# The end of an attention and FFN block: output products of one step inside the next step's softmax, and the last norm in two pairs of tiles

## What is computed

```
Q = norm(x) @ Wq.T        K = ctx @ Wk.T        V = ctx @ Wv.T      (8 groups of 4 query heads)
scores = Q K * 128**-0.5, causal over 64 positions; probs = softmax(scores)
x = x + tanh(g_xattn) * (probs @ V) @ Wd.T
w = (unpacked 6-bit qweight - zero_point) * scale
x = x + tanh(g_ffn) * (norm(x) @ w.T + bias)
norm(x) = (x - mean) / sqrt(var + 1e-5), over 512 features
```

## Time and profile before

| | |
|---|---|
| median of three executions | 1109.43 us |
| the profiled execution, and its span | 1111.87 us, 1110.1 us |
| mean granted TensorE clock | 0.986 of 2.4 GHz |
| TensorE busy | 1043.2 us, 94% of the span |
| VectorE busy | 717.6 us, 65% |
| ScalarE busy | 487.9 us, 44% |
| GpSimd busy | 238.3 us, 21% |

### The profile page before, as it was taken

The page is one execution under the profiler, slowest core; times in us unless marked ns, Lnnn a source line. Parts: engine busy times, 40 slices in busy tenths (PEclk is TensorE's granted clock), DMA queues, the critical chain, the costliest instruction groups (busy, mean ns, idle before and its releaser), DMA issues.

```text
span 1110.1 us, 20245 instructions
## 1 busy us (share of the span) xinstructions
PE 1043.2 (94%) x8054; PEld 589.1 (53%) x8054; DVE 717.6 (65%) x1347; ACT 487.9 (44%) x937; POOL 238.3 (21%) x242
## 2 busy tenths in 40 slices
PE   5899999998999999999999999999999999999974
PEld 3455545554455555455555555555555555555532
DVE  6856666567667666665566676656567656655567
ACT  5756674684624334244435323254433532333322
POOL 1535564457513110110002110110000300000012
PEclk9999999999999999999999999999999999999987
DMA  7746545432462342333222443322233233331101
GB/s 265 235 144 248 202 145 168 142 124 98 130 210 79 132 148 100 114 115 114 90 78 82 171 153 114 115 81 63 105 115 115 96 115 114 115 115 58 58 19 57
DMA packets 64251, 137.10 MB, mean 124 GB/s; under 512 B 5408, under 2 KB 38176, under 8 KB 53536
## 3 DMA queue, kind: packets, MB, share of 16 engines
q1 hardware_dynamic: 64160, 135.81, 35.8%
HBM read 93.85 MB, written 25.17 MB: 107 GB/s over the span
## 4 chain that ended last, share of the span: by engine, by line
PE 79%; DVE 9%; ACT 5%; issue 3%; POOL 0%; DVEq 0%; ACTq 0%; POOLq 0%
PE pa L1127 34%; PE py L1127 30%; PE av L1234 5%; PE ps L1201 3%; PE py L1284 3%; PE pp L1217 2%; PE av L1269 1%; DVE sc L838 1%; DVE row_max L842 1%; DVE sc L844 1%; ACT junk L537 1%; DVE sc L855 1%; DVE q L798 1%; ACT pT L636 1%; ACT junk L547 1%
## 5 line engine op out<-in xcount | busy, mean ns | idle before, releaser
L1127 PE MATMUL pa<-xT,wq 128*128 128x512 f16 x1536 | 347.3, 380 | 7.9 <-DVE q L798 5.2
L1127 PE MATMUL py<-wd,att 128*128 128x512 f16 x1536 | 351.4, 381 | 0.9 <-ACT att L643 0.9
L1127 PEld LDWEIGHTS pa<-xT,wq 128*128 128x128 f16 x1536 | 144.2, 98 | 180.3 <-issue 20.9
L1127 PEld LDWEIGHTS py<-wd,att 128*128 128x128 f16 x1536 | 149.0, 99 | 164.8 <-issue 5.2
L877 DVE SCALAR_TENSOR_TENSOR xacc<-py,f_y,xacc 128x512 f32<-128x512 f32 x128 | 96.1, 750 | 160.8 <-PE py L1127 160.8
L598 ACT ACTIVATE q<-pa 128x512 f16<-128x512 f32 x128 | 75.7, 592 | 248.2 <-PE pa L1127 248.2
L643 ACT ACTIVATE att<-av 128x256 f16<-128x256 f32 x256 | 80.9, 385 | 160.7 <-PE av L1234 160.3
L868 DVE SCALAR_TENSOR_TENSOR att<-av,att 128x256 f16<-128x256 f32 x256 | 93.5, 416 | 78.7 <-ACT att L643 78.6
L798 DVE SCALAR_TENSOR_TENSOR q<-pa,q 128x512 f16<-128x512 f32 x128 | 87.4, 683 | 20.6 <-ACT q L598 20.6
L1127 PE MATMUL pa<-wv,cT 128*128 128x128 f16 x1536 | 96.2, 219 | 0.0
L1127 PEld LDWEIGHTS pa<-wv,cT 128*128 128x128 f16 x1536 | 89.8, 98 | 0.9
(11 more groups left out here) (110 smaller groups left out, 1103.2 us busy)
## 6 DMA issues: line engine op xcount, KB each, us to landing
wq<-kept_q SPq DMA_DIRECT2D x24, 1024.0 KB, 7.9
wd<-kept_d SPq DMA_DIRECT2D x24, 1024.0 KB, 4.8
v_dup<-v_nat SPq DMA_DIRECT2D x128, 128.0 KB, 2.4
raw_d<-in_wdT SPq DMA_DIRECT2D x8, 1024.0 KB, 8.4
kept_q<-wq SPq DMA_DIRECT2D x8, 1024.0 KB, 8.8
kept_d<-wd SPq DMA_DIRECT2D x8, 1024.0 KB, 4.8
raw_q<-in_wqT SPq DMA_DIRECT2D x7, 1024.0 KB, 5.3
wk<-kept_k SPq DMA_DIRECT2D x24, 256.0 KB, 7.7
```

The lines of the kernel that those rows point to most:

```text
L1127: last = pe.matmul(out, stationary(a, i), moving(b, i), start=(i == 0 and (a, b) == PASSES[0]), stop=(i == count - 1 and (a, b) == PASSES[ ...
```

## The change

Step 30 no longer runs its output products (y_unit, y_part); they stand between the parts of step 31's softmax on TensorE and VectorE. Step 31's own output weights get a place of their own, wd_last (the second half of raw_d), and a load of their own (back_d_last), issued ahead of back_d(30). The FFN units of block 2 (LATE, tiles 8 to 11) use the banks pa instead of py, and their scaled products go to xs (the second half of raw_q) instead of xn; two stand in step 31 around the attention units, two behind its last output product. The last norm is done in two pairs of tiles (ln_stats_of, rstd_here with a slice), the first pair between output products 1 and 2 of step 31. ScalarE, POOL and the transpositions and FFN units of block 3 go by the same pairs; the stores of block 2 and 3 stand together at the end of SyncE's list. The core of the diff (indentation cut by eight):

```diff
+xs = raw_q[:, 1, :, :, :].rearrange("p h k n -> p h (k n)")
+wd_last = raw_d[:, 1, :, :].rearrange("p h n -> p (h n)").bitcast(F16).rearrange(
+    "p (c h n) -> p c h n", c=2, h=HPG)
...
+LAST = STEPS - 1
+LATE = tuple(range((BLOCKS - 2) * TILES, (BLOCKS - 1) * TILES))
 def ffn_of(n):
     g, tb = n % GROUPS, n // GROUPS
-    if n == STEPS - 1:
-        return BLOCKS - 2
     if g == 1 and 0 < tb < BLOCKS - 1:
         return tb - 1
...
+    def back_d_last():
+        sp.wait_ge(wd_lo, 4 * GROUPS)
+        sp.dma_start(wd_last.rearrange("p c h n -> p (c h n)"), kept_d[GROUPS - 1]).then_inc(d_last, 16)
...
+        if n == LAST - 1:
+            back_d_last()
+        if GROUPS <= n < LAST:
             back_d(n)
...
-    for t in FFN_DVE:
+    for t in LATE + FFN_DVE:
...
         pool.wait_ge(xr_ok, t + 1)
         pool.wait_ge(f_scaled, t + 1)
-        pool.tensor_tensor(acc(t), acc(t), xn[:, t % TILES, :], ALU.add).then_inc(out_pool, 1)
+        part = xs[:, t % TILES, :] if t in LATE else xn[:, t % TILES, :]
+        pool.tensor_tensor(acc(t), acc(t), part, ALU.add).then_inc(out_pool, 1)
...
-    for t in FFN_DVE:
-        residual(t)
+    for pair in (0, 2):
+        for t in LATE[pair:pair + 2]:
+            ffn_add(t)
+        for t in FFN_DVE[pair:pair + 2]:
+            residual(t)
...
-    for t in range(t0, t0 + TILES):
-        ln_hi(t, True)
-    for t in range(t0, t0 + TILES):
-        ln_out(t)
+    for pair in (t0, t0 + 2):
+        for t in (pair, pair + 1):
+            ln_hi(t, True)
+        for t in (pair, pair + 1):
+            ln_out(t)
...
+    def ln_stats_of(call, pair):
+        before = 4 * call + 2 * pair
+        two = slice(pair, pair + 2)
+        for t in (pair, pair + 1):
+            dve.wait_ge(bn_ok, TILES * call + t + 1)
+            dve.bn_aggr(mv[:, t, :], bn[:, t, :]).then_inc(mv_ok, 1)
+        dve.wait_ge(mv_ok, TILES * call + pair + 2)
+        dve.tensor_scalar(var_e[:, two], mv[:, two, 1], LN_EPS, None, ALU.add).then_inc(seed_ok, 1)
+        dve.tensor_scalar(half_var[:, two], mv[:, two, 1], LN_EPS, -0.5, ALU.add, ALU.mult).then_inc(seed_ok, 1)
+        dve.wait_ge(seed_ok, before + 2)
+        dve.tensor_scalar(rs_bits[:, two], var_e[:, two].bitcast(I32), 1, None,
+                          ALU.logical_shift_right).then_inc(seed_ok, 1)
+        dve.wait_ge(seed_ok, before + 3)
+        dve.tensor_scalar(rs[:, 0, two].bitcast(I32), rs_bits[:, two], -1.0, float(RSQRT_MAGIC),
+                          ALU.mult, ALU.add).then_inc(seed_ok, 1)
+        dve.wait_ge(seed_ok, before + 4)
+    def rstd_here(before, at):
         count = before
...
+        if 1 < call < len(NORMS) - 1 and NORMS[call - 1][0] == 2:
             dve.wait_ge(out_pool, NORMS[call - 1][1] * TILES + at + 1)
-        if call == len(NORMS) - 1:
-            dve.wait_ge(out_pool, (BLOCKS - 2) * TILES + at + 1)
...
-        dve.tensor_tensor(xn[:, t % TILES, :], py[t % 2][:, :], ff_rows[:, SCALE_ROW, :],
+        bank, part = (pa, xs) if t in LATE else (py, xn)
+        dve.tensor_tensor(part[:, t % TILES, :], bank[t % 2][:, :], ff_rows[:, SCALE_ROW, :],
                           ALU.mult).then_inc(f_scaled, 1)
...
-            y_part(n, j)
+            if n < LAST - 1:
+                y_part(n, j)
             if g == GROUPS - 1:
...
+    n, last = LAST, len(NORMS) - 1
+    scores(n, 0)
+    y_part(n - 1, 0)
+    scores(n, 1)
+    normalise(n, 0)
+    y_part(n - 1, 1)
+    p_part(n, 0)
+    normalise(n, 1)
+    y_part(n - 1, 2)
+    p_part(n, 1)
+    y_part(n - 1, 3)
+    ffn_scaled(LATE[0])
+    av_part(n, 0)
+    av_part(n, 1)
+    ffn_zero(LATE[0])
+    ffn_scaled(LATE[1])
+    ffn_zero(LATE[1])
+    y_part(n, 0)
+    ln_bn(last, 0)
+    av_part(n, 2)
+    y_part(n, 1)
+    ln_bn(last, 1)
+    av_part(n, 3)
+    ln_stats_of(last, 0)
+    rstd_here(10, slice(0, 2))
+    ln_norm(TILES * last)
+    ln_norm(TILES * last + 1)
+    y_part(n, 2)
+    ln_bn(last, 2)
+    ln_lo(TILES * last)
+    ln_lo(TILES * last + 1)
+    y_part(n, 3)
+    ln_bn(last, 3)
+    ln_stats_of(last, 2)
+    rstd_here(20, slice(2, 4))
+    ln_norm(TILES * last + 2)
+    ln_norm(TILES * last + 3)
+    ffn_scaled(LATE[2])
+    ffn_scaled(LATE[3])
+    ln_lo(TILES * last + 2)
+    ln_lo(TILES * last + 3)
+    ffn_zero(LATE[2])
+    ffn_zero(LATE[3])
+    for pair in (0, 2):
+        for t in FFN_DVE[pair:pair + 2]:
+            ffn_zero(t)
+        for t in FFN_DVE[pair:pair + 2]:
+            ffn_scaled(t)
+            ffn_result(t)
...
+            elif n == LAST:
+                pe.wait_ge(d_last, 16)
...
-                lambda b, h: wd[:, b, h, :], HPG).then_inc(y_mm, 1)
+                lambda b, h: (wd_last if n == LAST else wd)[:, b, h, :], HPG).then_inc(y_mm, 1)
...
-        pe.wait_ge(y_ok, min(4 * n, 4 * STEPS))
+        if t == LATE[0]:
+            pe.wait_ge(k_hi, STEPS)
+            pe.wait_ge(k_lo, STEPS)
+        elif t == LATE[1]:
+            pe.wait_ge(v_hi, STEPS)
+            pe.wait_ge(v_lo, STEPS)
+        elif t not in LATE:
+            pe.wait_ge(y_ok, 4 * n)
         wait(pe, f_scaled, t - 1)
...
+        bank = pa if t in LATE else py
...
+        if n == LAST - 1:
+            av_unit(n, 2)
+            av_unit(n, 3)
+            continue
...
+    n, t0 = LAST, TILES * (len(NORMS) - 1)
+    score_unit(n, 0)
+    y_unit(n - 1, 0)
+    score_unit(n, 1)
+    y_unit(n - 1, 1)
+    y_unit(n - 1, 2)
+    p_transpose(n, 0)
+    y_unit(n - 1, 3)
+    p_transpose(n, 1)
+    ffn_unit(LATE[0], n)
+    av_unit(n, 0)
+    av_unit(n, 1)
+    ffn_unit(LATE[1], n)
+    y_unit(n, 0)
+    av_unit(n, 2)
+    y_unit(n, 1)
+    av_unit(n, 3)
+    y_unit(n, 2)
+    y_unit(n, 3)
+    ffn_unit(LATE[2], n)
+    ffn_unit(LATE[3], n)
+    for pair in (0, 2):
+        ln_transpose(t0 + pair, 4 * STEPS)
+        ln_transpose(t0 + pair + 1, 4 * STEPS)
+        ffn_unit(FFN_DVE[pair], STEPS)
+        ffn_unit(FFN_DVE[pair + 1], STEPS)
```

More of the change, by code:

```diff
@@ L147, in build @@
         q_back, k_back, v_back, d_back = pair("q_back"), pair("k_back"), pair("v_back"), sem("d_back")
+        d_last = sem("d_last")
         ff_ld = sem("ff_ld")
@@ L917, in rstd_here @@
                 for i in range(3):
-                    y = rs[:, i, :]
-                    chained(dve.tensor_tensor(rs_t[:, :], y, half_var[:, :], ALU.mult))
-                    chained(dve.tensor_tensor(rs_u[:, :], rs_t[:, :], y, ALU.mult))
+                    y = rs[:, i, at]
+                    chained(dve.tensor_tensor(rs_t[:, at], y, half_var[:, at], ALU.mult))
+                    chained(dve.tensor_tensor(rs_u[:, at], rs_t[:, at], y, ALU.mult))
                     if i < 2:
-                        chained(dve.scalar_tensor_tensor(out=rs[:, i + 1, :], in0=rs_u[:, :], scalar=1.5, in1=y,
+                        chained(dve.scalar_tensor_tensor(out=rs[:, i + 1, at], in0=rs_u[:, at], scalar=1.5, in1=y,
                                                          op0=ALU.add, op1=ALU.mult))
-                chained(dve.tensor_scalar(rs_u[:, :], rs_u[:, :], 1.5, XN_SCALE, ALU.add, ALU.mult))
-                chained(dve.tensor_tensor(rstd[:, :], rs_u[:, :], rs[:, 2, :], ALU.mult))
+                chained(dve.tensor_scalar(rs_u[:, at], rs_u[:, at], 1.5, XN_SCALE, ALU.add, ALU.mult))
+                chained(dve.tensor_tensor(rstd[:, at], rs_u[:, at], rs[:, 2, at], ALU.mult))
             def ln_norm(t):
@@ L1031, in _ @@
             dve.wait_ge(const_ok, 3)
-            for n in range(STEPS):
+            for n in range(LAST):
                 g, tb, m = n % GROUPS, n // GROUPS, n + 1
-                ahead = m < STEPS
                 call = norm_of(n)
@@ L1047, in _ @@
                         split_wq(1, h)
-                if ahead:
-                    q_part(m, 0)
-                if ffn is not None and not ahead:
-                    ffn_scaled(t0)
+                q_part(m, 0)
                 scores(n, 1)
                 normalise(n, 0)
-                if ahead:
-                    q_part(m, 1)
+                q_part(m, 1)
                 if ffn is not None:
-                    ffn_scaled(t0 if ahead else t0 + 1)
+                    ffn_scaled(t0)
                 p_part(n, 0)
                 normalise(n, 1)
-                if ahead:
-                    q_part(m, 2)
+                q_part(m, 2)
                 if ffn is not None:
-                    ffn_scaled(t0 + 1 if ahead else t0 + 2)
+                    ffn_scaled(t0 + 1)
                 p_part(n, 1)
-                if ahead:
-                    q_part(m, 3)
+                q_part(m, 3)
                 if ffn is not None:
-                    ffn_scaled(t0 + 2 if ahead else t0 + 3)
-                if ffn is not None and ahead:
+                    ffn_scaled(t0 + 2)
                     ffn_scaled(t0 + 3)
-                if ahead:
-                    k_part(m)
+                k_part(m)
                 if call is not None and g == 0:
@@ L1104, in _ @@
                     ln_stats(NORMS.index((1, tb + 1)))
```

(14 more changed lines are left out.)

49 lines of the change are left out of this document (14 added, 35 removed).

## The result

The changed kernel takes 1095.4 us (median of 4; 1092.9 to 1095.56) against 1109.43 (median of 4), a ratio of 0.9867 with a 95% interval of 0.9849 to 0.9884: 14.0 us, 1.3% faster. The forecast was 1094.2 (range 1091.2 to 1099.0). Run once more beside the experiments it took 1095.73 against 1110.51, ratio 0.9865 (0.9850 to 0.9880).

What follows compares the result with a forecast made beforehand. TensorE, busy 94% of the span, left about 20 us idle and some lower clock in the last 60 us. VectorE's last instruction moves from 1107.66 to 1092.5, so 1109.43 - 15.2 = 1094.2 us, range 1091.2 to 1099.0.

Steps and rivals of the forecast that it cites:

- The softmax stretch: Step 31 on TensorE: step 30's products fill the softmax waits, so the last output product ends 14.0 us earlier, at 1068.1.
- FFN unit 12's wait: TensorE at the end: 5.4 us idle for unit 10's f_scaled, then unit 12 at 1.2 GHz, 3.41 us.
- The norm in pairs: Last norm on VectorE: ten small instructions paid twice, 2 us more work, with VectorE the bound of the new end.
- Contention: End of the kernel: POOL's two adds and two residuals slow VectorE's ffn_zero and ffn_result by 2.3 us.
- rival (a): End of the kernel: all six POOL instructions hold VectorE, 6.4 instead of 3.4 us; 3.0 later, 1097.2 us; chance 0.20.
- Two chains of nearly one length: End of the kernel: TensorE's chain leads to an end at 1091.0, VectorE's to 1092.5 with POOL's slowing.
- The sum: Whole end: VectorE's last instruction moves from 1107.66 to 1092.5, 15.2 us less, last store unchanged behind it.
- (b): Step 31's softmax isn't covered: TensorE waits 2 us more and the clock falls; 5 to 6 later, 1099.5 us; chance 0.13.
- (c): End of the kernel: the 10.5 us of idle time only move and nothing is gained, 1109.4 us; chance 0.03.
- (d): Clock falls in step 31's softmax and stays low to the end: 15.2 gained, 19.5 lost, 1113.7 us; chance 0.02.
- The waits for d_last, k and v: Step 31 on TensorE: added waits for the extra weight load and for units 8 and 9's inputs cost 0.

Runs made afterwards that it cites:

- the filler: 24 unused matmuls put in TensorE's four softmax waits, against the kernel with step 30's output products back in step 30: 1105.98 us, 0.9950 of the kernel before.
- POOL cut: Changed kernel with POOL's last four instructions working on one column instead of 512, other columns left out: 1093.50 us, 0.9845 of the kernel before.
- early ffn_zero: Changed kernel with block 2's four ffn_zero together in VectorE's pause before FFN unit 8's result: 1095.00 us, 0.9855 of the kernel before.
- again: The changed kernel, nothing further altered, run once more beside the experiments: 1095.73 us, 0.9865 of the kernel before.

## Why the prediction was right, point by point

- **The softmax stretch: right.** Forecast: last output product 14.0 us earlier, ended at 1068.1, or 1067.4 with the 0.69 us by which this profile entered the stretch earlier; measured 1067.31 (the next product starts at 1067.15). Counted from the yardstick it is 14.1 us earlier, 30.98 instead of 45.10. I had TensorE waiting about 1.0 us, 0.8 of it for p_part 0; it waited 0.31, with 2.4 GHz throughout as taken. That the gain is idle time and clock, and the products' place its cause, is shown: putting the products back costs 12.5, the filler returns 1.9 of it. As in the forecast, 3.5 us are the two FFN units put behind.
- **FFN unit 12's wait: right.** 5.4 us forecast, 5.33 measured; the two units at 5.7 against 5.83.
- **The norm in pairs: right that it costs a second chain and that VectorE is the bound of the new end.** The chain of statistics took 2.92 us (1063.78 to 1066.70) against 2.85 taken. What the text didn't say is how little the pairs bring on top of the moved products: 0.33 us of stretch.
- **Contention: right in the sum, not in its parts.** 2.3 taken, 2.58 measured, and 0.91 for ln_lo (2.20 - 1.29) against 1.1. I took 2.3, above the middle, because ffn_result is of the kind of ln_lo, and had no row for ffn_zero. It came the other way round: ffn_result lost only 0.28 each (0.56 in all), and ffn_zero 2.02, as two of four took 1.75 us instead of 0.75. That 2.3 comes so near is in part luck. The rule of the Trainium skill (page "SBUF — State Buffer", section "Who interferes with whom") for two SBUF inputs bears on ffn_zero too, and the trace agrees: 1.75 us beside POOL and 0.75 without. The page's exemption of instructions with at most one SBUF input has a condition that the prediction left out: it holds outside the 2-port perf modes. ln_norm, with one SBUF tensor, was held in the trace (1.49 us instead of 0.54 beside POOL), y_part (0.74) and bn_stats (0.69) were not. The sign that I named for rival (a), ffn_zero over 1.2 us, came true for these two. But its price, all six of POOL's instructions at 6.4 us, is out: 3.5 us in all, because y_part, bn_stats and ffn_scaled, which were not held, lie between, and ffn_result lost little.
- **Two chains of nearly one length: right.** Forecast: by TensorE's chain the end would be at 1091.0, by VectorE's at 1092.5, 1.5 us apart. Measured: TensorE's last product ended 1.3 us before VectorE took it up. With POOL cut, TensorE held VectorE by 0.87 us (53.00 against 52.13).
- **The sum.** 15.2 us forecast for the stretch, 15.93 measured. Of the 0.8 us by which VectorE was ahead of the forecast (counted from the yardstick), 0.3 is there at the first statistics, and 0.4 more comes up to the first late ffn_zero, where a pair of ffn_scaled and a pair of undisturbed ln_lo took 1.20 us instead of 1.3 each and the stall of the first pair's ln_lo was smaller. The medians moved by 14.0 and 14.8, less than the stretch. Profile against profile it closes (1111.87 - 1095.26 = 16.61, that is 15.93 and 0.69 at the entry). For the medians it isn't shown where the rest lies, since the median executions weren't profiled; in the profiles the entry varies, and the clock inside the stretch. The forecast took the gain of one profiled execution off a median of others, and that it came within 1.2 us is partly luck.
- **Rivals (b), (c), (d):** the clock did not fall in the softmax, idle time did not move there, nothing became slower. The waits for d_last, k and v cost nothing: TensorE's list shows no pause before the products that carry them.

## What to carry to other kernels

Where the last step has no successor to fill its waits, hold back independent work of the step before (here output products) and lay it between the parts of the last step. Once the fastest way through is on another engine, waits and clock on TensorE are worth nothing as long as it stays ahead of that engine (here by 1.3 us), and moving an instruction on the bound engine out of the end is worth only what a neighbour doesn't take back, as POOL did with the early ffn_zero. Measure a change of the end from a row that both kernels reach in the same way, not from the start.

## What the runs showed of the hardware

- The clock behind a pause doesn't follow from the pause's length. Behind 2.81 and 2.73 us of idle the same FFN unit took 3.51 us in one kernel and 1.90 in the other. Behind 5.32 or 5.33 us, with TensorE's list the same in four kernels, units 12 and 13 took 5.83, 5.76, 5.33 and 5.08 us (changed kernel, again, POOL cut, ffn_zero early). So where TensorE ends last, a stretch from one execution is uncertain by some 0.5 us.
- Taking the bank wait away moved TensorE's idle time from before units 12 and 13 to before 14 and 15, where the lower clock was nearer to the end. It gained nothing (54.71 to 54.92). That it costs (53.00 to 53.56 with POOL cut) isn't shown: the difference is no larger than that uncertainty, and the medians are equal (1093.50 and 1093.46).
- POOL suffers as well: its add of 512 columns took 1.26 us in the earlier trace rows and 1.7 beside ffn_zero (3.38 for two).
- Two executions of one list of instructions entered the end stretch up to 6.0 us apart (1034.33 to 1040.33 us over all profiles), and nearly all of it comes from the first 300 us. With VectorE's instructions matched one by one, the profiles are up to 4.1 us apart at 77 us. Two steps follow, of 1.6 to 1.7 us in six profiles between 170 and 203 us and of 0.5 us in seven between 257 and 288 us. The first stands in just those profiles whose clock between 100 and 200 us is 0.98 and not 1.00, the second in just those where it is so between 200 and 300 us. The first such stretch in the changed kernel (columns as in the earlier trace rows):

```profile
170.50:173.80 3.30, 3.30 (x9) 1.22 (x8) 0.00 (x0) 0.00 (x0) 0.00 (x0) 0.50 0.61 138
```

From 321 us to the stretch no profile moved against another by more than 0.3 us. What sets the first 77 us wasn't looked into.
